# Experts' second products with rows as weights, turned through HBM, with the first attention batch begun behind them

## What is computed

```python
# third sublayer: rows in 32 groups of 16 (ne), 64 experts (16 x 4)
grouped = x.reshape(..., 32, 16, 512)
logits  = einsum('btd,des->btes', grouped, controller) + tie
perm    = (logits == max(logits, axis=t))            # each expert takes one row of each group
sel     = einsum('btd,btes->besd', grouped, perm)
inner   = relu(einsum('besd,desf->besf', sel, f1) + bias)   # 512 -> 64 per expert
inter   = einsum('besf,esfd->besd', inner, f2)              # 64 -> 512 per expert
x       = x + einsum('besd,btes->btd', inter, perm)         # combination
# fourth sublayer, per batch b of 8, 16 heads of 32
q = norm(x) @ Wq.T ; k = ctx[b] @ Wk.T ; v = ctx[b] @ Wv.T
x = x + (softmax(q k / sqrt(32)) v) @ Wp.T + bp
```

## Time and profile before

| | us |
|---|---|
| median of 3 runs | 1179.06 (1177.03 to 1179.46) |
| profiled execution, its own time | 1176.5 |
| its span | 1174.7 |
| TensorE busy | 1133.5 (96%) |
| TensorE weight loads busy | 854.5 (73%) |
| DVE, ACT, POOL busy | 619.1, 432.8, 333.6 |

### The profile page before, as it was taken

How to read it: one execution, slowest core, us unless ns; L and a number is a source line. 1 busy time by engine, 2 the same in 40 slices (tenths; PEclk the granted TensorE clock), 3 DMA queues, 4 the chain that set the end, 5 groups by cost and what they waited for, 6 DMA issues and landing times.

```text
span 1174.7 us, 35100 instructions
## 1 busy us (share of the span) xinstructions
PE 1133.5 (96%) x16122; PEld 854.5 (73%) x16122; DVE 619.1 (53%) x977; ACT 432.8 (37%) x824; POOL 333.6 (28%) x364
## 2 busy tenths in 40 slices
PE   8988999999899999999999999999999999999896
PEld 5433454488688789788788888888888878856573
DVE  2011259555412655655655655655655565486667
ACT  1010153124333434443533534433533543435343
POOL 0000000025000242533344333424434342364512
PEclk9899999999999999999999999999999999999999
DMA  9999981254001101101100200200111110320000
GB/s 369 363 415 409 394 324 60 87 202 165 26 18 59 38 20 60 38 20 60 38 21 25 74 21 25 74 20 25 45 41 34 38 38 20 132 83 2 21 1 37
DMA packets 27620, 115.75 MB, mean 99 GB/s; under 512 B 2504, under 2 KB 3016, under 8 KB 22352
## 3 DMA queue, kind: packets, MB, share of 16 engines
q1 hardware_dynamic: 27472, 113.50, 26.1%
HBM read 112.44 MB, written 1.05 MB: 97 GB/s over the span
## 4 chain that ended last, share of the span: by engine, by line
PE 88%; DVE 5%; DMA 4%; issue 2%; ACT 1%; POOL 0%; SPq 0%; DVEq 0%; ACTq 0%; POOLq 0%
PE SB L431 50%; PE SB L422 7%; PE SC L1211 6%; PE SB L1240 4%; DMA R<-in_ctx_t 3%; PE SB L1276 2%; PE SC L996 2%; PE SC L1020 2%; PE SB L1084 1%; PE SB L1097 1%; PE SC L1203 1%; PE SB L1259 1%; PE SB L415 1%; PE SC L873 1%; PE SC L1220 1%
## 5 line engine op out<-in xcount | busy, mean ns | idle before, releaser
L1723 ACT COPY R<-SB 64x512 f32<-64x512 f32 (+1 forms) x224 | 116.3, 519 | 190.9 <-PE SB L431 189.0
L431 PE MATMUL SB<-high,whigh 128*128 128x512 f32 (+2 forms) x512 | 180.4, 352 | 1.0 <-ACT Z L444 1.0
L1526 DVE TENSOR_REDUCE LN<-SC 128x64 f32<-128x768 f32 x128 | 116.6, 952 | 119.8 <-PE SC L1211 119.7
L431 PE MATMUL SB<-high,wlow 128*128 128x512 f32 (+2 forms) x512 | 178.5, 349 | 0.0
L431 PE MATMUL SB<-low,whigh 128*128 128x512 f32 (+2 forms) x512 | 177.1, 346 | 0.0
L431 PE MATMUL SB<-wlow,high 128*128 128x512 f32 (+1 forms) x416 | 165.5, 398 | 0.0
L431 PE MATMUL SB<-whigh,high 128*128 128x512 f32 (+1 forms) x416 | 164.2, 395 | 0.0
L431 PE MATMUL SB<-whigh,low 128*128 128x512 f32 (+1 forms) x416 | 164.0, 394 | 0.0
L745 POOL TENSOR_TENSOR added<-LN 128x768 f32<-128x768 f32 x32 | 58.7, 1834 | 249.8 <-ACT LN L1755 249.8
L745 POOL TENSOR_TENSOR added<-Z 128x768 f32<-128x768 f32 x32 | 58.6, 1831 | 243.2 <-ACT Z L1755 243.2
L431 PEld LDWEIGHTS SB<-high,whigh 128*128 128x128 f32 x512 | 97.0, 189 | 13.6 <-issue 1.4
(11 more groups left out here) (235 smaller groups left out, 1843.1 us busy)
## 6 DMA issues: line engine op xcount, KB each, us to landing
R<-in_ctx_t SPq DMA_DIRECT2D x32, 1024.0 KB, 6.0
R<-in_ctx SPq DMA_DIRECT2D x8, 3072.0 KB
R<-in_ctx_t SPq DMA_DIRECT2D x16, 644.0 KB, 7.0
R<-in_f SPq DMA_DIRECT2D x4, 2048.0 KB, 15.1
R<-in_f SPq DMA_DIRECT2D x1, 8192.0 KB, 25.0
R<-in_ctx_t SPq DMA_DIRECT2D x12, 512.0 KB, 3.6
R<-in_Wk SPq DMA_DIRECT2D x3, 1024.0 KB, 10.3
R<-in_Wv SPq DMA_DIRECT2D x3, 1024.0 KB, 8.8
```

Of the source, the lines that this page charges most:

```text
L431: last = pe.matmul(out_, lhs[a][:, k, :], rhs[b][:, k, :], start=n == 0, stop=n == 3 * NC - 1)
L1526: inc(dve.tensor_reduce(tops[:, r * T:(r + 1) * T], sc_head[:, :, r, 0:6 * T].rearrange("p g (a q) -> p q g a", q=T), AX.XY, ALU.max), "ha ...
L1723: last = act.copy(keys[nu][64 * half:64 * half + 64, pairs, first * P:first * P + full], src[:, :, 0:full])
```

## The change

Four things are changed together.

1. **`inner`**: each half takes only its own expert's rows, 32 moving columns in place of 64; the zeroing of `inner` and the block copies go.
2. **`inter`**: the rows are now the weights (64 partitions x 32 columns) and `f2s` moves (64 partitions x 512 columns). Eight such matmuls, two row halves by four column groups of the array, fill two banks; there are 8 such pairs of banks. The result has (four experts' pairs, group) on the partitions and the output dimension along the row.
3. **The turn**: in place of 64 transposes, each pair of banks is written to a scratch tensor in HBM (8 stores of 512 KB), and when all are there it is read back in the order that the combination wants (4 loads of 1 MB, Wq4 in between).
4. **`FIRST4`**: keys and values of piece 0 stand ahead of and between the combinations (`c`), turns of normed rows (`t`) and queries (`q`), in banks of `SC` (`ring4`), and all of these are steps of the table now. Piece 0 and Wk4 are loaded when `inner` 2 is filled. The high part of Wv4 is made by POOL, the low part of piece 0 by DVE behind its last copy of `inter`. The idle-time matmuls from `inner` on are gone.

Also `three_passes` goes through the four parts of the contraction in each pass now, where it went through the passes in each part; the order of the passes is high by high, low by high, high by low. This holds for all such products of the kernel. Regions of `R` are laid out anew, and the tie row has another shape.

```diff
-FIRST4 = [("h", 0), ("q", 0)] + EARLY4 + [("g", 0)]
+FIRST4 = [K0[0], K0[1], K0[2], ("c", 0), K0[3], ("c", 1), ("t", 0), ("v", 0), ("c", 2), ("t", 1), ("v", 1), ("c", 3),
+          ("t", 2), ("v", 2), ("t", 3), ("v", 3), ("h", 1), ("q", 0)] + REST4 + [("g", 0)]
...
+        def ring4(steps, n):
+
+            return SC[:, n * 512:(n + 1) * 512] if steps is FIRST4 else BK[n]
...
             for n in within:
-                k, (a, b) = n // 3, ((0, 0), (0, 1), (1, 0))[n % 3]
+                k, (a, b) = n % NC, ((0, 0), (1, 0), (0, 1))[n // NC]
...
+        def low_part(eng, low_, raw, high, name):
+
+            for c in range(NC):
+                last = eng.tensor_tensor(low_[:, c, :], raw[:, c, :], high[:, c, :].bitcast(F32), ALU.subtract)
+            inc(last, name)
...
-            sp.wait_ge(*filled("inner", 3))
-            inc(sp.dma_start(wraw[0], natural(Wk4)), "wk4_in", 16)
-            inc(sp.dma_start(wraw[1], natural(Wv4)), "wv4_in", 16)
-            sp.wait_ge(*filled("inter", 15))
-            inc(sp.dma_start(wq4, natural(Wq4)), "wq4_in", 16)
-            inc(sp.dma_start(bprow, bp4.unsqueeze(0).to_broadcast([P, D])), "bp_in", 16)
+            sp.wait_ge(*filled("inner", 2))
+            inc(sp.dma_start(wraw[0], natural(Wk4)), "wk4_in", 16)
+            load_chunk(0, 0)
+            sp.wait_ge(*filled("inner", 3))
+            inc(sp.dma_start(wraw[1], natural(Wv4)), "wv4_in", 16)
+
+            turned = scratch.rearrange("a (r m j s) d -> m j (a r) (s d)", r=2, m=EM, j=4)
+            for m in range(EM):
+                for r in range(2):
+                    sp.wait_ge(*readout("inter", 2 * m + r))
+                inc(sp.dma_start(turned[m], inter[:, m].rearrange("p s d -> p (s d)")),
+                    "scratch_first" if m < 2 else "scratch_out", 16)
+            sp.wait_ge(sem("scratch_first"), 16 * 2)
+            sp.wait_ge(sem("scratch_out"), 16 * (EM - 2))
+            rows = scratch.rearrange("a p d -> p a d")
+            for tt in range(NT):
+                inc(sp.dma_start(intern[:, 4 * tt:4 * tt + 4, :], rows[:, 4 * tt:4 * tt + 4]), f"intern_in{tt}", 16)
+                if tt == 1:
+                    inc(sp.dma_start(wq4, natural(Wq4)), "wq4_in", 16)
...
-            sp.wait_ge(*filled("intert", 15))
+            sp.wait_ge(*filled("y3", NT - 1))
...
-                            last = pe.matmul(bk[64 * r:64 * r + 64, j * 64:(j + 1) * 64],
+                            last = pe.matmul(bk[64 * r:64 * r + 64, j * G:(j + 1) * G],
                                              f1s[q][:, k, j * P + 64 * r:j * P + 64 * r + 64],
-                                             sel[:, k, 2 * (8 * q + j):2 * (8 * q + j) + 2, :],
-                                             start=k == 0, stop=k == NC - 1)
+                                             sel[:, k, 2 * (8 * q + j) + r, :], start=k == 0, stop=k == NC - 1)
...
-                            last = pe.matmul(bk[64 * r:64 * r + 64, j * 64:(j + 1) * 64],
-                                             f2s[:, 8 * q + j, c * P + 64 * r:c * P + 64 * r + 64],
-                                             inner[:, 8 * q + j, :], start=True, stop=True)
...
+            for m in range(EM):
+                if m % 2 == 0:
+                    pe.wait_ge(*readout("inner", m // 2))
+                bks = [open_bank(pe, "inter", 2 * m + r) for r in range(2)]
+                for j in range(4):
+                    for r in range(2):
+                        last = pe.matmul(bks[r][32 * j:32 * j + 32, :], inner[64 * r:64 * r + 64, 4 * m + j, :],
+                                         f2s[64 * r:64 * r + 64, 4 * m + j, :], start=True, stop=True)
+                        if j == 3:
+                            last.then_inc(filled("inter", 2 * m + r)[0], 1)
...
-            normed(pe, 3, combination, (1.8, 1.2, 0.5, 1.8))
-            running(pe, 1.0)
...
             evacuate(dve, "d", "inter", inter_dst)
...
+            dve.wait_ge(sem("high"), 1)
+            low_part(dve, cols(low_r[0]), cols(low[0]), cols(high_r[0]), "split_first")
...
-            for w, name in enumerate(("wk4_in", "wv4_in")):
-                evacuate(act, "a", "inter", inter_dst, range(8 * w, 8 + 4 * w))
-                act.wait_ge(sem(name), 16)
-                inc(act.copy(whigh[w], wraw[w]), "whigh")
-            evacuate(act, "a", "inter", inter_dst, range(12, 16))
+            act.wait_ge(*filled("inner", 3))
+            act.wait_ge(sem("wk4_in"), 16)
+            inc(act.copy(whigh[0], wraw[0]), "whigh")
+            evacuate(act, "a", "inter", inter_dst, range(0, 8))
+            act.wait_ge(sem("chunk_in0"), 16)
+            inc(act.copy(high_r[0], low[0]), "high")
+            evacuate(act, "a", "inter", inter_dst, range(8, 16))
```

More of the change, by code:

```diff
@@ L485, in build @@
         rows_low = cols(float32r("rows_low", LN_AT))
-        inner = Z[:, 1, :].rearrange("p (a k) -> p a k", k=2 * G)
+        inner = Z[:, 1, 0:1024].rearrange("p (a g) -> p a g", g=G)
         sel = R3.rearrange("p a c n -> p (a c n)").rearrange("p (c e g) -> p c e g", c=NC, g=G)
-        intert = view(24576, 8192, NC, G, E)
-        intern = view(16384, 8192, G // 2, D)
+        inter = view(24576, 8192, EM, 2, D)
+        intern = view(6656, 8192, G // 2, D)
+        scratch = nc.dram_tensor("inter_rows", (G // 2, P, D), F32).ap()
         MP = M + 1
@@ L658, in load_batch @@
             def load_batch(b):
-                for c in range(KC):
+                for c in range(b == 0, KC):
                     if c >= 2:
@@ L708, in split_weight @@
             def split_weight(pool, w, high, low, name):
-                inc(pool.tensor_copy(high, w), name)
+                for c in range(NC):
+                    last = pool.tensor_copy(high[:, c, :], w[:, c, :])
+                inc(last, name)
                 pool.wait_ge(sem(name), 1)
-                inc(pool.tensor_tensor(low, w, high.bitcast(F32), ALU.subtract), name)
+                for c in range(NC):
+                    last = pool.tensor_tensor(low[:, c, :], w[:, c, :], high[:, c, :].bitcast(F32), ALU.subtract)
+                inc(last, name)
             inc(pool.memset(causal[:, :], 0.0), "causal")
@@ L730, in _ @@
                 spread_choice(pool, tt, "permb_p")
-            for w in range(2):
-                pool.wait_ge(sem("whigh"), w + 1)
-                inc(pool.tensor_tensor(wlow[w], wraw[w], whigh[w].bitcast(F32), ALU.subtract), "wlow")
+            pool.wait_ge(sem("whigh"), 1)
+            low_part(pool, wlow[0], wraw[0], whigh[0], "wlow")
+            pool.wait_ge(sem("wv4_in"), 16)
+            for c in range(NC):
+                last = pool.tensor_copy(whigh[1][:, c, :], wraw[1][:, c, :])
+            inc(last, "whigh_v")
+            pool.wait_ge(sem("whigh_v"), 1)
+            low_part(pool, wlow[1], wraw[1], whigh[1], "wlow")
             pool.wait_ge(sem("wq4_in"), 16)
@@ L943, in probabilities_out1, with steps4 @@
                     inc(copy(pt1[0:MR, MF, :], bk[0:MR, 0:P]), f"read1_{g}")
-        def steps4(eng, run):
+        def steps4(eng, run, then=None):
             run(FIRST4, None, None)
+            if then:
+                then()
             for b in range(B - 1):
@@ L1088, in _ @@
                 last.then_inc(filled("inner", q)[0], 1)
-            running(pe, 1.6)
             pe.wait_ge(sem("f2_in"), 16)
-            for q in range(4):
-                pe.wait_ge(*readout("inner", q))
-                for c in range(NC):
-                    bk = open_bank(pe, "inter", 4 * q + c)
-                    for j in range(8):
-                        for r in range(2):
-                            last = pe.matmul(bk[64 * r:64 * r + 64, j * 64:(j + 1) * 64],
-                                             f2s[:, 8 * q + j, c * P + 64 * r:c * P + 64 * r + 64],
-                                             inner[:, 8 * q + j, :], start=True, stop=True)
-                    last.then_inc(filled("inter", 4 * q + c)[0], 1)
@@ L1106, in _ @@
             pe.wait_ge(sem("permx"), 2)
             def combination(tt):
-                for i in range(4):
-                    pe.wait_ge(*readout("intert", 4 * tt + i))
+                pe.wait_ge(sem(f"intern_in{tt}"), 16)
                 bk = open_bank(pe, "y3", tt)
@@ L1510, in run4 @@
                 for kind, x in steps:
-                    if kind == "v":
+                    if kind == "c":
+                        norm(dve, 3, add_row("y3"), tiles=range(x, x + 1))
+                    elif kind == "t":
+                        norm_low(dve, 3, x, norm3_low)
+                    elif kind == "v":
                         n = tile_keys(x)
@@ L1518, in run4 @@
                         split_low(x)
+                        if steps is FIRST4 and x == KC - 1:
+                            dve.wait_ge(sem("bp_in"), 16)
+                            for tt in range(NT):
+                                inc(dve.tensor_tensor(X[:, tt, :], X[:, tt, :], bprow, ALU.add), "xbp")
```

166 lines of the change are left out of this document (81 added, 85 removed).

## The result

| | before | after |
|---|---|---|
| median, us | 1179.26 (1177.03 to 1181.24, 4 runs) | 1194.55 (1191.35 to 1196.43, 4 runs) |
| profiled execution, its own time | 1176.5 | 1191.35 |
| its span | 1174.7 | 1189.4 |

The ratio is 1.0127, 95% interval 1.0095 to 1.0159: slower by 1.3%, where 1.7% faster was forecast. The prediction was wrong in its sign, and the forecast of the span (1155.0) is missed by 34.4 us.

What follows compares the result with a forecast made beforehand. TensorE was taken to bound the kernel. Its stage before piece 1's keys was to shrink from 90.9 to 69.8 us, 21.1 less, minus 1.4 for the clock: 19.7 gained, forecast 1159 us, range 1152 to 1168 at 0.80.

Steps and rivals of the forecast that it cites:

- the trip: Storing `inter`'s result to HBM and loading it back: stores landed at 281, first load at 286.1 us.
- the trip is slower than its neighbours: Rival on the HBM stores and loads: 2.0 us a store gives 1164, half rate with slower loads 1174; chance 0.20.
- A trip three times as slow: Rival in the HBM stores and loads making the kernel slower; shares chance 0.06 with a costly order of passes.
- The trip is just hidden, and whatever more it loses goes nearly whole to the time: HBM loads against TensorE's wants at the combinations: spare time 0.4, 1.3, -0.2 and 1.2 us, further delay lengthening the run.
- `inner` stays at 15.0: First products: 512 records bound by weight loads, so halving the moving columns leaves some 15.0 us.
- the rival that it halves: Rival in `inner`: 7 us at the scores' rate, keys about 5.8 us sooner, 1153 us in total; chance 0.15.
- `inter` 1.0 us a pair: Eight matmuls filling a pair of banks take 1.0 us, 8 us in all, with eight array tiles in use.
- The splits of 0.62 us: DVE's split of piece 0 before the first keys: four pieces of 0.62 us, done at 278.3.
- The clock: TensorE's clock falls once in two new idle stretches of 2.8 and 3.2 us, charged at 1.4 us.
- The clock falls in `inner`: Rival: TensorE's clock falls in `inner` and stays down, up to 10 us lost, 1169 us; chance 0.06.
- Order of passes at nothing: Reordering passes over 2784 products costs nothing; rival of 10 ns more each gives 1187, sharing chance 0.06.
- What is behind 338.7 stands in the same order afterwards: Work from piece 1's keys (338.7 us before) is unchanged, so the earlier stage's difference carries to the end.

Runs made afterwards that it cites:

- The narrow weights: Changed kernel with sixteen 256 KB stores of 32 partitions, plus `inner` weights of 32 columns for 64, half its columns left out: 1165.51 us, one run.
- the one with everything earlier: Changed kernel with sixteen 256 KB stores of 32 partitions, plus earlier Wk4 and piece 0 loads, piece 0 cast and split before `inter`'s copies: 1171.42 us.

## Why the prediction was wrong

- **The failed step** is in the trip: "Stores of 512 KB at the 380 GB/s of the last stores are 1.4 us each, 11 us for eight." At the 105 GB/s measured they take 5.0 us each, and the eight 45.2 from the first issue to the last landing, where 281 was forecast and 312.4 came. The 380 GB/s came from stores whose outermost count is 128 partitions; this one's is 4. What stands in its place: the count of engines by 26 GB/s each, 105 for four, as the runs with counts of 2, 4 and 32 show. The rival "the trip is slower than its neighbours" was there, but its worst price was half the rate of the stores, and it named the strides and the untried scratch tensor, not the count that decides. "A trip three times as slow" held a share of 0.06 with the order of passes; the stores were 3.6 times as slow.
- **"The trip is just hidden, and whatever more it loses goes nearly whole to the time"**: right. The first load landed 32.0 us later than forecast (318.1 for 286.1); 5.9 were taken up by keys that started and ran late, 0.4 by the spare time, and 25.7 became the wait. With the stores mended and nothing else changed the wait is 0 to 1.6.
- **`inner` stays at 15.0**: right, 15.4 (246.97 to 262.39), and with it the rival that it halves falls. The narrow weights show the cause: 17.3 ns a record for 30.5.
- **`inter` 1.0 us a pair**: right at full clock (32 records, two pairs, in 1.95 to 2.26); row halves do work side by side. The waits at ACT were forecast at 2.8 us and about 1, and were 2.56 and 1.19.
- **The splits of 0.62 us** were mis-sized: 1.15 beside POOL, 2.1 us of the 3.6 by which the keys came late, counted from `inner`. The rows 6 that they were priced by come from a stretch where POOL is idle (304 to 307 us).
- **The clock** was charged with 1.4 us, one fall. It fell three times: 1.4 in `inter` (64 records in 5.34 us for 3.9), 3.1 in the keys, 1.6 behind the trip. "The clock falls in `inner`" did not come true in the changed kernel, but in the one with everything earlier it did, behind two waits of 0.78 and 1.18 us, and cost 5.6.
- **Order of passes at nothing**: right (0.9995).
- **"What is behind 338.7 stands in the same order afterwards"**: nearly; 2.6 us came on top, mostly unexplained and within what profiles of the other versions differ by (3.4).
- With the one step put right (the 32-partition stores) the gain is 14.5 us where 19.7 was forecast. From the first `inner` to piece 1's keys 76.4 us pass there, where 69.8 and 1.4 for the clock were forecast. Of the 6.6 over 69.8, 3.8 are late keys (2.8 of it the split, which took 5.24 us), 2.2 are the clock in the keys, and 0.6 small waits. So the rest of the sum was right in its mechanism and short by 5.2 us.

## What to carry to other kernels

Before a transfer is priced by a row's GB/s, compare the outermost count of both access patterns with that row's: a low DMA share beside a busy queue (0.26 at 105 GB/s) is the sign that few engines work, and splitting the transfer by that dimension costs a line. A round trip through HBM in place of transposes pays only if independent work fills it; here the filling was worth 21.6 us, up to 7 of them by the clock. When a wait is shortened, look at what is next: edits that each did what they should (splits, casts, idle-time matmuls, four keys ahead) brought the keys 6.0 us forward, and only 2.2 of these reached the end of the stage; the rest went into a wait of 3.65 for the trip and what it did to the clock, and into the wait for the last norm.

## Not expected of the hardware

- Stores of 32 partitions move 241 to 265 GB/s with the engines 0.86 to 0.95 busy, whether 128 or 256 KB each; stores of 128 partitions 393 GB/s.
- DVE's subtraction of 128 x 512 takes 0.62 us alone and 1.15 beside POOL's of the same kind. POOL's takes 1.48 then (5.91 for four), and 1.25 in the version that keeps them apart (4.99).
- Waits "issue" of 0.8 to 2.4 us inside long runs of small matmuls, after each 127 to 148 records, with and without data transfers beside them; and a clock of 0.50 for 12 us in a stretch where TensorE is busy all the time, but with weight loads (12.00 of 12.00 us), while three waits of 2.35, 1.41 and 1.13 us in the run with narrow weights left it at 1.00.
